# A selective-scan block and a ternary feed-forward layer: B's SiLU taken token-major from one shared turn

## The reference

```
u = layernorm(x)
z0, x0, xBC, dt = split(u @ W_in.T)          # 512, 512, 512+16+16, 8 channels
xBC = silu(causal_conv4(xBC) + conv_b)       # x: 8 heads of 64; B, C: 16 states, shared by the heads
dt = softplus(dt + dt_bias);  A = -exp(A_log)
h = exp(dt*A) * h + dt * x[..., None] * B    # per head, step by step over the tokens
y = h @ C + D * x
y = layernorm(y) * ln_gamma + ln_beta
y = sigmoid(y @ W_gate.T + b_gate) * y
x = x + concat(silu(z0) * x0, y) @ W_out.T
f = layernorm(gelu(layernorm(x) @ ternary(W_fc).T)) * ln_w + ln_b
x = x + f @ ternary(W_proj).T
```

## Time and profile before

| | us |
|---|---|
| median of 3 runs | 1075.17 (1074.15 to 1076.78) |
| the profiled execution | 1074.0 |
| its span in the trace | 1072.2 |
| PE busy | 1021.1 (95%), 11470 matmuls |
| DVE busy | 935.9 (87%) |
| ACT busy | 933.3 (87%), of it 200.1 in 156 table loads |
| POOL busy | 489.9 (46%) |
| granted TensorE clock, mean | 0.994 |

### The profile page before, as it was taken

One profiled execution on the slowest core, in us unless ns is written; L12 is line 12 of the kernel. 1 busy time (PEld: TensorE's weight loads), 2 busy tenths in 40 slices (PEclk: granted clock), 3 DMA queues, 4 the chain that ended last, 5 costly groups with the idle time before them and its releaser, 6 DMA issues.

```text
span 1072.2 us, 29421 instructions
## 1 busy us (share of the span) xinstructions
PE 1021.1 (95%) x11470; PEld 652.2 (61%) x11470; DVE 935.9 (87%) x1992; ACT 933.3 (87%) x1620; POOL 489.9 (46%) x590
## 2 busy tenths in 40 slices
PE   5759999999999999999999999999999999999996
PEld 3344757566675756667576665756667575665674
DVE  5999998989998999998989988998989899875666
ACT  4869598999989888999898999998999999978785
POOL 1445444543545435443644552455434425443733
PEclk9989999999999999999999999999999999999999
DMA  7423242555564554555455356545555553452658
GB/s 257 102 53 80 66 88 52 100 103 89 101 119 93 100 84 97 105 97 114 73 124 90 84 99 110 107 76 106 84 90 119 81 110 62 94 96 58 125 110 163
DMA packets 303659, 106.20 MB, mean 99 GB/s; under 512 B 271904, under 2 KB 299808, under 8 KB 303520
## 3 DMA queue, kind: packets, MB, share of 16 engines
q1 hardware_dynamic: 303520, 104.31, 49.3%
HBM read 28.38 MB, written 8.91 MB: 35 GB/s over the span
## 4 chain that ended last, share of the span: by engine, by line
PE 69%; DVE 14%; ACT 7%; issue 5%; DMA 3%; SPq 1%; POOL 1%; DVEq 0%; ACTq 0%; POOLq 0%
PE bank L413 41%; PE bank L673 8%; PE bank L685 7%; PE bank L613 3%; PE bank L594 2%; DVE cv L1081 2%; PE bank L622 2%; PE bank L519 2%; DVE sty L1214 1%; ACT L183 1%; DMA x<-in_x 1%; PE bank L568 1%; DVE yT L1206 1%; DVE st L1036 1%; DVE Xd L1143 1%
## 5 line engine op out<-in xcount | busy, mean ns | idle before, releaser
L413 PE MATMUL bank<-xnT,win 128*128 128x512 f16 x1152 | 275.5, 383 | 3.5 <-DVE th L1169 1.2
L183 ACT ACT_TABLE_LOAD x156 | 200.1, 1283 | 2.8
L413 PEld LDWEIGHTS bank<-xnT,win 128*128 128x128 f16 x1152 | 110.2, 99 | 121.7 <-issue 5.3
L413 PE MATMUL bank<-yhl,wg 128*128 128x512 f16 x768 | 176.5, 381 | 0.6 <-DMA yhl<-ynh 0.5
L1391 POOL TENSOR_TENSOR caty<-tg,caty 128x512 f16<-128x512 f32 x64 | 83.0, 1297 | 189.6 <-ACT caty L890 189.5
L1081 DVE SCALAR_TENSOR_TENSOR cv<-bank,cws,cv 128x511 f32<-128x511 f32 (+2 forms) x192 | 142.9, 746 | 6.4 <-ACT tail L790 1.4
L673 PE MATMUL bank<-wfc,x3T 128*128 128x512 f16 x512 | 130.0, 380 | 1.7 <-issue 1.3
L685 PE MATMUL bank<-wpj,hT 128*128 128x256 f16 x1024 | 122.4, 273 | 6.3 <-DMA hT<-hb 5.6
L413 PEld LDWEIGHTS bank<-yhl,wg 128*128 128x128 f16 x768 | 73.2, 98 | 87.5 <-issue 5.4
L1386 POOL TENSOR_TENSOR yT<-yhl 128x512 f32<-128x512 f16 x64 | 78.4, 1237 | 96.8 <-DMA yhl<-ynh 96.8
L1395 POOL TENSOR_TENSOR cat<-sz,cat 128x512 f16<-128x512 f32 x64 | 83.8, 1311 | 81.2 <-ACT cat L902 68.0
(11 more groups left out here) (167 smaller groups left out, 2037.8 us busy)
## 6 DMA issues: line engine op xcount, KB each, us to landing
x<-in_x SPq DMA_DIRECT2D x31, 512.0 KB, 4.6
out_y<-x SPq DMA_DIRECT2D x15, 512.0 KB, 3.2
crep<-c_rows SPq DMA_DIRECT2D x16, 256.0 KB
hT<-hb SPq DMA_TRANSPOSE x128, 3.3
caty<-in_wg SPq DMA_DIRECT2D x1, 1024.0 KB, 8.1
x<-in_wout SPq DMA_DIRECT2D x1, 1024.0 KB, 9.7
hT<-in_wfc SPq DMA_DIRECT2D x1, 1024.0 KB, 10.4
hb<-in_wpj SPq DMA_DIRECT2D x1, 1024.0 KB, 7.1
```

Source lines behind the costliest of these rows:

```text
L183: self.eng.preload_act_table_set(self.table)
L413: m = eng.matmul(b, lhs(p, k), rhs(q, k), start=(n == 0), stop=(n == len(seq) - 1))
```

## The change

The transposes `turn_b` are gone, with their semaphore `be_mm`. A new ACT step `u` (`silu_b`) reads raw B, token-major, from the bank of `turn_u`, after DVE has copied dt from it, and writes SiLU(B) to a new tile `bt` in SBUF. DVE's `b_suffix` reads `bt` and does in one instruction of 512 columns what it did in two of 256. The bank of `turn_u` is free again after ACT's `u`, not after DVE's copy. The state-major SiLU (ACT `b`) stays, for the products with C. All five tables are new. The core of the diff:

```
 PE_ORDER = (
-    "X00 X01 c02 c03 u04 c05 B06 c07 c00 z01 m02 z04 c13 s05 c17 b00 x02 c11 x05 v03 g024 x07 u13 e00 x03 c15 c12 "
...
+    "X00 X01 c02 c03 u04 c05 c06 c07 B00 m01 z02 z03 c15 c14 x06 x07 u11 s05 c16 e00 g025 x04 x07 c12 q054 O00 "
...
+        bt = sb("bt", [P, NCH, 16])
...
             def turn_u(i, n, at):
...
-                gives(at, u_cp, i + 1)
+                gives(at, bt_act, i + 1)
...
-            def turn_b(i, n, at):
-                b = take(at)
-                pe.wait_ge(bc_act, i + 1)
-                for q in range(2):
-                    m = eng.transpose(b[:, q * P:(q + 1) * P], bcs[:, i % 2, chunk(q)], ident)
-                m.then_inc(be_mm, 1)
-                gives(at, be, i + 1)
...
             def silu_bc(i, n):
...
-                act.wait_ge(be_mm, i - 1)
...
+            def silu_b(i, n):
+                (b,) = bank["u", i, 0]
+                act.load("Silu")
+                act.wait_ge(u_cp, i + 1)
+                act.wait_ge(be, i)
+                eng.activation(bt[:, :, :].rearrange("p (h q) r -> p h q r", h=2), turned(b, 0, 16), ACT.Silu).then_inc(bt_act, 1)
...
             def b_suffix(i, n):
-                (b,) = bank["b", i, 0]
-                dve.wait_ge(be_mm, i + 1)
+                dve.wait_ge(bt_act, i + 1)
...
-                for k in range(2):
-                    op = eng.tensor_tensor(BE[:, 2 * k:2 * k + 2, :, :],
-                                           turned(b, 0, 16)[:, k].unsqueeze(2).broadcast_to([P, 2, 8, 16]),
-                                           esuf[:, 2 * k:2 * k + 2, :].unsqueeze(3).broadcast_to([P, 2, 8, 16]), ALU.mult)
-                op.then_inc(be, 1)
+                eng.tensor_tensor(BE[:, :, :, :], bt[:, :, :].unsqueeze(2).broadcast_to([P, NCH, 8, 16]),
+                                  esuf[:, :, :].unsqueeze(3).broadcast_to([P, NCH, 8, 16]), ALU.mult).then_inc(be, 1)
```

More of the change, by code:

```diff
@@ L214, in build @@
         ht_hi, ht_lo = ([sem(f"{n}{k}") for k in range(2)] for n in ("ht_hi", "ht_lo"))
-        conv_mm, u_mm, cum_mm, x_mm, ec_mm, es_mm, be_mm, g_mm, st_mm, seg_mm, car_mm, own_mm, yt_mm, gb_mm, x0t_mm = (
-            sem(n) for n in ("conv_mm u_mm cum_mm x_mm ec_mm es_mm be_mm g_mm st_mm seg_mm car_mm own_mm yt_mm gb_mm "
+        conv_mm, u_mm, cum_mm, x_mm, ec_mm, es_mm, g_mm, st_mm, seg_mm, car_mm, own_mm, yt_mm, gb_mm, x0t_mm = (
+            sem(n) for n in ("conv_mm u_mm cum_mm x_mm ec_mm es_mm g_mm st_mm seg_mm car_mm own_mm yt_mm gb_mm "
                              "x0t_mm").split())
@@ L220, in build @@
             sem(n) for n in "gate_mm z_mm x0_mm out_mm fc_mm proj_mm ones_mm csum_mm r0_mm".split())
-        a_step, xn, xn_hi, conv_ev, bc_act, xs, dt_exp, dt_ln, cum_hi, cum_lo, ec_exp, es_exp, e_exp = (
-            sem(n) for n in "a_step xn xn_hi conv_ev bc_act xs dt_exp dt_ln cum_hi cum_lo ec_exp es_exp e_exp".split())
+        a_step, bt_act, xn, xn_hi, conv_ev, bc_act, xs, dt_exp, dt_ln, cum_hi, cum_lo, ec_exp, es_exp, e_exp = (
+            sem(n) for n in "a_step bt_act xn xn_hi conv_ev bc_act xs dt_exp dt_ln cum_hi cum_lo ec_exp es_exp e_exp".split())
         yn, yf_ev, y_hi, tanh, yg_hi, z_silu, cat_hi, gelu, h_mu, h_sq, hn_hi, x2_hi = (
@@ L690, in _ @@
             STEPS = {"X": turn_first, "O": ones_sum, "C": column_sums, "R": bias_rows, "B": gate_bias, "c": conv, "u": turn_u, "m": cum, "x": turn_x,
-                     "e": grow, "s": suffix, "b": turn_b, "g": gram, "t": states, "q": seg, "r": carried, "w": own,
+                     "e": grow, "s": suffix, "g": gram, "t": states, "q": seg, "r": carried, "w": own,
                      "y": turn_y, "G": gate, "z": skip_z, "v": skip_x, "o": out, "f": fc, "p": proj}
```

2 lines of the change are left out of this document (1 added, 1 removed), and 231 rows, old and new, of tables (ACT_ORDER, DVE_ORDER, PE_ORDER, POOL_ORDER).

## The result

The changed kernel takes 1079.52 us, the median of 15 runs (1076.25 to 1085.71); the kernel before took 1075.20 beside it (15 runs). The ratio is 1.0045, 95% interval 1.0032 to 1.0059: slower by 0.45%, where 1071.4 us, in a range of 1066 to 1078, was forecast. The profiled execution took 1079.52 us, with a span of 1077.5 against 1072.2.

What follows compares the result with a forecast made beforehand. TensorE was taken as the bound, 99% busy from 93 to 910 us. Terms: -3.5 TensorE, -0.3 gaps, 0 for start, end and VectorE: 3.8 us less, 1075.17 to 1071.4 us, range 1066 to 1078.

Steps and rivals of the forecast that it cites:

- TensorE, minus 3.5: Two transposes per block removed from TensorE, counted as time where it is full: 3.5 us less, bounds 3.2 and 3.7.
- The gaps, minus 0.3 (bounds -7.1 to +3): TensorE's 7.1 us idle between 93 and 910 us: 0.3 gained; bounds all 7.1 gained or 3 lost.
- The start, 0 (-3.5 to +9.5): Up to the first gate product: 1.0 gained and 0.9 owed, taken as 0; bounds 3.5 gained or 9.5 lost.
- ScalarE and VectorE: 16 SiLUs more, ten table loads fewer: ScalarE 9.1 us lighter; VectorE 1 to 3 us less; mostly hidden under TensorE.
- The end, 0: Last 32 us, block 15's feed-forward: same alternation, TensorE's 9.0 us idle stay; 0, plus or minus 1.
- Given back: Rival: gaps of the new order, such as waits for `u`'s bank or a late start, eat the saving; 1074 to 1076, chance 0.15.
- The late `segL`: Rival: at the start, the delay from ACT `5` to the gate comes through; up to +6 us, 1081, chance 0.18.
- The sign to watch: Prediction is wrong if the middle, 93 to 910 us, has more than 10 us of TensorE idle; about 7 expected.

Runs made afterwards that it cites:

- 2: Changed kernel with the loads of x, residual and copies of C cut to 64 columns in later blocks: 1073.46 us, 0.9977 of the kernel before.
- 3: Kernel before the change, with the loads of x, residual and copies of C cut to 64 columns in later blocks: 1073.65 us, ratio 0.9982.
- 8: Changed kernel whose `turn_u` issues its two transposes twice, as dead work: 1080.28 us, 1.0032 of the kernel before.
- 15: Old tables with `turn_b` removed, and `turn_u` issuing its two transposes twice: 1082.41 us, 1.0051 of the kernel before.
- 9: Changed kernel with 32 small products (64 TensorE records) added ahead of the first conv: 1087.18 us, 1.0101 of the kernel before.
- 10: Changed kernel with 63 small products (126 TensorE records) added ahead of the first conv: 1084.42 us, 1.0082 of the kernel before.
- 4: Changed kernel whose sync queue in blocks 2 and 3 waits for step w before loading x and what follows: 1081.73 us, 1.0063 of the kernel before.
- 7: Changed kernel with the x loads of blocks 5 and 6 moved later, one of them without a wait: 1075.60 us, 1.0002 of the kernel before.
- 13: Changed kernel with the x loads of blocks 5 to 15 moved later in the sync queue: 1089.83 us, 1.0126 of the kernel before.
- 11: Changed kernel with step w's four words spread apart by other dense words in blocks 2 to 14: 1086.36 us, 1.0104 of the kernel before.

## Why the prediction was wrong

- **TensorE, minus 3.5.** The work was sized rightly, as far as 2 and 3 can tell: 3.7 us of busy time fell with small loads. That it would be time was wrong. Putting it back cost nothing that shows in the new order (8), and in the old one about 2 us, within the intervals (15). "PE is full, so work taken from it is time" holds only if what takes its place isn't a wait.
- **The gaps, minus 0.3 (bounds -7.1 to +3).** This is the step that failed, by size and by kind. Idle time in the middle rose by 9.2 us, three times the bound: 10.7 more of issue waits, all but 0.5 at the ends of instruction packets, less 1.1 on data. I had called issue time a part "that no order changes". It is what the order changed: the packets' ends lie at nearly the same places of r and w in blocks 2 and 3 as before (80 and 24 records into r, 74 and 24 before), but three loads are now issued as r begins, and in block 2 the next packet starts to move 4.9 us after TensorE has reached the end of the last one, where it was 0.8. With the lower clock behind the two longest waits the middle lost 3.3 us instead of gaining 3.8.
- **The start, 0 (-3.5 to +9.5).** It cost 1.8. `segL` at 40.89 (forecast 41.7), `Y` at 66.46 (66.4), `bc`'s taps of block 2 from 74.36 to 75.87 (76.0) came close, `Y` in part by luck: VectorE was ready at 65.6 and waited 0.84 for w, which had waited 1.12 for its instructions at 64.92. The last `n` began at 89.33 where it was to end at 88.3: VectorE had waited 1.52 for ScalarE's `ynh` at 88.12. Then the six matmuls ahead of the gate waited 0.71 for `EM` at 93.37, and the gate came at 94.67 for 91.9. I had priced none of these waits and no clock: 23.8 of the first 95 us were at 1.2 GHz, 10.2 before. What the clock alone cost here isn't shown.
- **ScalarE and VectorE.** Minus 12.1 us on ScalarE (9.1 forecast), the SiLU of `bt` 222 ns (230). The trace has 147 loads for 156, nine fewer and 11.5 us, where ten and 12.8 were forecast, so 4.2 us more than forecast fell elsewhere. VectorE's multiply is 701 ns, not 620, and above the bound of 680; it is near the 681 of L1143. The time saved on both engines is hidden under TensorE.
- **The end, 0.** It held: the tail took 31.0 us for 30.8. Its last projections ran in part at the lower clock (5.32 us for 32 where two of before would take 3.8), but the waits ahead of them were shorter (1.16 and 2.21 us against 1.18, 2.87 and 0.66).
- **The rivals.** "Given back" had the right mechanism in kind, gaps of the new order, and too small a price (1074 to 1076); its own example, a wait for the bank of `u`, isn't what came. The late `segL` was not the cause. The sign to watch was named: a middle over 10 us idle. It was 16.3.

What is shown: the waits are at the ends of packets of instructions (148 of them end 1.2 to 2.0 us after a packet has moved, and 9 and 10 moved them to the matmul), and their size in blocks 2 and 3 hangs on the loads, which delay the packet (2, 4, 7). What stays open: why the removal pays nothing in the old order, where issue waits rose by only 1.7 us and data waits by 5.9, the longest 2.03; and why the shifted kernels 9 and 10, whose waits sum to nearly the same, are 2 to 6 us slower than the changed one in its two sets of runs.

## What to carry to other kernels

Read "issue" gaps by position: if they stand at equal counts of instructions in different kernels, and a packet of the instruction queue has just moved, the engine was waiting for its own instructions. In this kernel it helped to keep large loads away from a stretch of hundreds of tiny matmuls (7), as long as no other engine then waited for the data (4 and 13); putting longer matmuls between the small ones did not help (11). An engine at 99% says that removed work could be time; before counting it, look at what waits a new order can bring and what the clock does behind them. Compare a reordered kernel with small loads first: it tells whether the order or the traffic costs.
